# A transformer stack on one core: rounded output product within one turn, one buffer for the heads' outputs, Gelu from PSUM, keys copied once and placed by two transfers

## What is computed

```python
def attn_layer(x, Wqkv, qs, ksc, Wo):          # x is shift_tokens(x); 16 heads of 64
    q, k, v = heads(x @ Wqkv)
    q = rotary(l2norm(q) * qs);  k = rotary_inv(l2norm(k) * ksc)
    sim = einsum('bhwie,bhwje->bhwij', bq, bk2) * 8.0        # windows of 32, causal
    out = einsum('bhwij,bhwje->bhwie', softmax(mask(sim)), bv2)
    return out.reshape(b, n, 1024) @ Wo

def ffn_layer(x, g, bln, W1, b1, W2, b2):      # x is shift_tokens(x)
    xn = (x - mu) / jnp.sqrt(var + 1e-05) * g + bln
    a, gate = jnp.split(xn @ W1 + b1, 2, -1)    # 341 + 341
    return a * gelu(gate) @ W2 + b2
```

## Time and profile before

| what | value |
|---|---|
| median of 3 runs | 3024.75 us (3023.71 to 3027.78) |
| the profiled execution | 3025.93 us, its span 3024.1 us |
| busy in the span | PE 94%, DVE 79%, ACT 80%, POOL 70% |
| the layers | first projection matmul 406.2 us, last 2933.3 us |

### The profile page before, as it was taken

One profiled execution on the slowest core, in us unless ns is written; L12 is line 12 of the kernel. 1 busy time (PEld: TensorE's weight loads), 2 busy tenths in 40 slices (PEclk: granted clock), 3 DMA queues, 4 the chain that ended last, 5 costly groups with the idle time before them and its releaser, 6 DMA issues. The chain is left out here.

```text
span 3024.1 us, 90067 instructions
## 1 busy us (share of the span) xinstructions
PE 2847.9 (94%) x34784; PEld 1995.9 (66%) x34976; DVE 2396.9 (79%) x3168; ACT 2423.9 (80%) x3783; POOL 2114.6 (70%) x1517
## 2 busy tenths in 40 slices
PE   8799978999999999999999999999999999999995
PEld 7688856666666666666666666666666666666662
DVE  7899967887787888778788787877788787887872
ACT  5788858788887878888788888878888887888872
POOL 6767657777677777777777777777777776777760
PEclk9899989999999999999999999999999999999997
DMA  1000011100111010010001111000110100100002
GB/s 51 22 1 1 1 33 26 27 23 20 27 32 30 23 26 24 21 41 24 23 23 26 28 31 26 23 23 24 30 31 23 26 23 25 28 21 20 18 21 64
DMA packets 73039, 76.57 MB, mean 25 GB/s; under 512 B 23078, under 2 KB 46692, under 8 KB 72804
## 3 DMA queue, kind: packets, MB, share of 16 engines
q1 hardware_dynamic: 71780, 74.01, 9.5%
q10 hardware_dynamic: 1152, 1.20, 0.1%
HBM read 22.72 MB, written 2.10 MB: 8 GB/s over the span
## 5 line engine op out<-in xcount | busy, mean ns | idle before, releaser
L1313 POOL TENSOR_TENSOR qk_r<-qk_r,qk_t 128x1024 f32<-128x1024 f32 x384 | 917.9, 2391 | 549.9 <-DVE qk_r L1169 387.9
L776 PE MATMUL pa<-w_hi,xs_hi 128*128 128x512 f32 x1152 | 576.2, 500 | 41.1 <-DVE qk_r L1169 24.8
L1162 DVE TENSOR_REDUCE ss<-sq 128x16 f32<-128x1024 f32 x384 | 463.6, 1207 | 19.0 <-ACT sq L959 18.2
L1178 DVE TENSOR_TENSOR qk_t<-pa,rot 128x1024 f32<-128x1024 f32 x384 | 465.5, 1212 | 0.0
L1169 DVE TENSOR_TENSOR qk_r<-pa,rot 128x1024 f32<-128x1024 f32 x384 | 465.5, 1212 | 0.0
L804 PEld LDWEIGHTS px<-ident_sb,qk_r 128*128 128x128 f32 x3072 | 352.3, 141 | 164.6 <-issue 100.5
L776 PE MATMUL pa<-w_hi,xs_lo 128*128 128x512 f32 x1152 | 456.5, 396 | 0.0
L776 PE MATMUL pa<-w_lo,xs_hi 128*128 128x512 f32 x1152 | 454.6, 395 | 0.0
L804 PE MATMUL px<-ident_sb,qk_r 128*128 128x128 f32 x3072 | 402.8, 274 | 30.4 <-POOL qk_r L1322 14.4
L1012 ACT COPY kT<-px 64x1024 f32<-64x1024 f32 x384 | 385.2, 1003 | 34.5 <-PE px L804 29.8
L1322 POOL TENSOR_TENSOR qk_r<-qk_r,inv 128x1024 f32<-128x1024 f32 x192 | 365.9, 1906 | 43.8 <-ACT inv L996 43.5
(11 more groups left out here) (142 smaller groups left out, 5344.4 us busy)
## 6 DMA issues: line engine op xcount, KB each, us to landing
pT<-prT SPq DMA_DIRECT2D x768, 64.0 KB, 2.0
w_part<-in_Wqkv SPq DMA_DIRECT2D x40, 192.0 KB, 2.7
wo<-in_Wo SPq DMA_DIRECT2D x6, 512.0 KB, 4.5
c_h<-in_x SPq DMA_DIRECT2D x4, 512.0 KB, 9.9
o_x<-in_x SPq DMA_DIRECT2D x8, 256.0 KB, 4.8
out<-o_out SPq DMA_DIRECT2D x8, 256.0 KB, 4.3
w<-in_W SPq DMA_DIRECT2D x6, 341.0 KB
spare<-in_Wqkv SPq DMA_DIRECT2D x1, 1536.0 KB, 6.3
```

Source lines behind the costliest of these rows:

```text
L776: last = pe.matmul(pa[(u + c) % 2][:, half * 512:half * 512 + 512], x[:, j * P:(j + 1) * P], w[:, at], start=(k == 0), stop=(k == 2))
L1162: dve.reduce_sum(ss[:, c, :], heads(sq[:]), AX.X).then_inc(s[sum_sem], 1)
L1178: dve.tensor_tensor(halves(qk_t[:, c, :]), halves(pa[(3 * j + c) % 2][:])[:, :, ::-1, :], table.unsqueeze(1).to_broadcast([P, HEADS, 2, DH ...
L1313: pool.tensor_tensor(qk_r[:, j % 2, c, :], qk_r[:, j % 2, c, :], qk_t[:, c, :], ALU.add)\
```

## The change

What it does, part by part:

- **Output product.** `Wo` is split once a layer in `wo_hi` (ACT, `round_wo`) and `wo_lo` (POOL, `rest_of_wo`). ACT's copy of the heads' outputs now rounds into `oT_hi`; a new step on DVE, `rest_of_outputs`, subtracts it from `px` and writes `oT_lo`. `project_out` has for each of its eight pairs of heads three float32r matmuls in place of one float32 matmul. `px` is free for the next transposes when both have read it (`oT_lo_ready`).
- **One buffer.** `oT_hi` and `oT_lo` hold one group in place of two. The values `v` and the rotated `qk_r` move into the room `spare` that `oT` had.
- **Gelu from PSUM.** The gate's three copies with bias become three Gelu with bias, straight from `pg`; the Gelu over `gt` goes. The tables for Gelu are asked for ahead of the first, those for exp and ln behind the third.
- **Keys.** ACT copies the transposed keys once, in full rows, to `k_both`; SP places them with two transfers of 64 rows and 4 KB a row, 256 KB each, into `kT`, whose layout is now halves first; `scores` waits for these.
- **Feed-forward.** The tiles `fsq`, `frs`, `fn` are one tile `fx`; the square is taken from PSUM; `scale_shift` moves from ACT to DVE.
- **Order.** Every engine's `body` is written anew. On PE `scores` comes after `project_q`, and `weigh_values` before `project_v`. `group_steps` writes out the first two groups of every layer. `w_part` has one buffer in place of two. PE no longer waits at the start for all cleared tiles.

The core of the diff, for all engines, SP and PE:

```diff
         def group_steps(eng, body, new_layer):
-            new_layer(0)
-            body(0, 0, 0)
-            body(1, 0, 1)
-            with eng.Fori(2, GROUPS) as g:
-                body(g, 0, g)
-            for l in range(1, DEPTH):
+            for l in range(DEPTH):
                 new_layer(l)
-                with eng.Fori(0, GROUPS) as g:
+                for g in range(2):
+                    body(g + l * GROUPS, l, g)
+                with eng.Fori(2, GROUPS) as g:
                     body(g + l * GROUPS, l, g)
...
+                def place_keys(i, j, back):
+
+                    n, _, live = tile(i, j, back)
+                    if live:
+                        sp.wait_ge(s["tk_out"], n + 1)
+                        wait_for(sp, s["scores_done"], n)
+                        for half in range(2):
+                            rows = slice(half * DH, (half + 1) * DH)
+                            sp.dma_start(kT[rows, half].rearrange("p h b j -> p (h b j)"), k_both[rows, :])\
+                                .then_inc(s["kT_ready"], 16)
+
                 def body(i):
                     for j in range(GT):
...
+                        place_probs(i, j, 3)
+                        place_keys(i, j, 1)
...
-                        wait_for(pe, s["pv_out"], n - 2)
+                        wait_for(pe, s["oT_lo_ready"], n - 2)
                         transposes(j, 0, "tq_done")
...
                         for hp in range(lo, hi):
-                            heads_out = oT[:, bass.ds(g % 2, 1), hp, :, :].rearrange("p o t n -> p (o t n)")
-                            last = pe.matmul(pg[:], wo[:, hp, :], heads_out, start=(hp == 0), stop=(hp == HP - 1))
+                            for k, (w, o) in enumerate(((wo_hi, oT_hi), (wo_hi, oT_lo), (wo_lo, oT_hi))):
+                                last = pe.matmul(pg[:], w[:, hp, :], o[:, hp, :, :].rearrange("p t n -> p (t n)"),
+                                                 start=(hp == 0 and k == 0), stop=(hp == HP - 1 and k == 2))
...
-                pe.wait_ge(s["mask_ready"], 2)
-                pe.wait_ge(s["zeroed"], 8)
                 group_steps(pe, body, lambda l: None)
```

The order of a turn on PE, as written now (turn by turn `j`):

```diff
+                        if j == 2:
+                            a_block(i, 2, 1)
                         project_q(i, j, l)
+                        if j == 0:
+                            subtract_mean(i, 2)
+                        scores(i, j, 2)
+                        transpose_q(i, j, 1)
+                        if j == 2:
+                            a_block(i, 2, 2)
                         if j == 1:
+                            gate_block(i, 2, 0)
+                        project_k(i, j, l)
+                        if j == 1:
+                            gate_block(i, 2, 1)
+                        if j == 3:
+                            project_out(i, 1, 0, HP // 2)
+                        transpose_k(i, j, 1)
+                        if j == 3:
+                            project_out(i, 1, HP // 2, HP)
+                        if j == 1:
+                            gate_block(i, 2, 2)
                         if j == 2:
+                            down(i, 2)
+                        if j == 0:
+                            variance(i, 2)
+                        weigh_values(i, j, 3, 1)
                         if j == 1:
+                            a_block(i, 2, 0)
                         project_v(i, j, l)
```

On ACT, the key copy, the Gelu and the order of a turn:

```diff
-                        for half in range(2):
-                            rows = slice(half * DH, (half + 1) * DH)
-                            act.copy(kT[rows, :, :, half, :].rearrange("p h b j -> p (h b) j"),
-                                     px[rows, :].rearrange("p (h j) -> p h j", j=S)).then_inc(s["tk_out"], 1)
...
+                        wait_for(act, s["kT_ready"], 32 * n)
+                        act.copy(k_both[:], px[:]).then_inc(s["tk_out"], 1)
...
-                        act.activation(gt[0:m, k, :], pg[0:m, :], ACT.Identity, bias=b1[0:m, 1, k:k + 1])\
+                        act.activation(gt[0:m, k, :], pg[0:m, :], ACT.Gelu, bias=b1[0:m, 1, k:k + 1])\
                             .then_inc(s["gate_out"], 1)
...
+                        if isinstance(g, int) and g == 1 and l < DEPTH and j == 0:
+                            round_wo(l)
+                        copy_v(i, j, 1)
+                        square_q(i, j, 0)
+                        log_norms(i, j, 1)
+                        inverse_norms(i, j, 1)
+                        if j == 0:
+                            shift_hi(i, 0, 1)
                         if j == 1:
+                            tables(i, 2, GELU)
+                        if j == 0:
+                            square_centred(i, 2)
+                        if j == 1:
+                            gate_gelu(i, 2, 0)
+                        copy_qT(i, j, 1)
+                        if j == 0:
+                            copy_centred(i, 2)
+                        square_k(i, j, 0)
+                        if j == 1:
+                            gate_gelu(i, 2, 1)
+                        copy_kT(i, j, 1)
+                        if j == 0:
+                            log_variance(i, 2)
+                            inverse_deviation(i, 2)
+                        if j == 1:
+                            gate_gelu(i, 2, 2)
+                            tables(i, 2, EXP_LN)
+                        exponentials(i, j, 2)
+                        if j == 3:
+                            shift_ffn(i, 1)
+                        if j == 1:
                             round_part(l, g)
...
+                        copy_oT(i, j, 3)
+                        floor_norms(i, j, 0)
```

On DVE the new step, and on POOL the order of a turn:

```diff
+                def rest_of_outputs(i, j, back):
+                    n, k, live = tile(i, j, back)
+                    if live:
+                        dve.wait_ge(s["pv_out"], n + 1)
+                        dve.tensor_tensor(oT_lo[:, :, k, :].rearrange("p h (r q) -> p r h q", r=2),
+                                          px[:].rearrange("p (r h q) -> p r h q", r=2, h=HP),
+                                          oT_hi[:, :, k, :].rearrange("p h (r q) -> p r h q", r=2).bitcast(F32), ALU.subtract)\
+                            .then_inc(s["oT_lo_ready"], 1)
...
+                        if j == 3:
+                            shift_lo(i, -1, 0)
+                        norm_keys(i, j, 1)
                         if j == 3:
                             rest_of_part(l, g)
...
+                        norm_scores(i, j, 2)
+                        if j == 1:
+                            shift_lo(i, 0, 1)
+                        rotate(i, j, 0, 0, "cos_q", "sin_q", "rot_q")
+                        rotate(i, j, 0, 1, "cos_k", "sin_k", "rot_k")
+                        norm_probs(i, j, 2)
```

450 lines of the change are left out of this document (204 added, 246 removed).

## The result

| what | before | after |
|---|---|---|
| median | 3025.34 us (4 runs, 3023.71 to 3027.78) | 2975.72 us (4 runs, 2974.20 to 2978.85) |
| span of the profiled execution | 3024.1 us | 2973.8 us |
| a group of the loop | 52.60 us | 51.63 us |

The ratio is 0.9838, 95% interval 0.9822 to 0.9853: 1.6% faster, 49.6 us. A second set of five runs on another chip gave 0.9840 (0.9827 to 0.9854). The forecast was 2930, 95 us less than before; its range held the time, its size was off by almost half. 0.97 us a group times 48 is 47 us, so nearly all of it was won in the loop; how it splits is at the end of the account of the prediction.

What follows compares the result with a forecast made beforehand. PE was taken as the bound, at 49.4 us of work a group. A group of 50.6, 2.0 less, gives 96 us (64 product, 32 order); with 1 off the start and 4 back, 2930 us, range 2885 to 2990.

Steps and rivals of the forecast that it cites:

- PE is the bound, and the product saves 1.34 us a group: Output product on PE: 24 float32r matmuls take 5.5 us where 16 records took 6.9; 64 us over 48 groups.
- ahead of each product with the values, with no releaser: PE's small waits before the values' matmuls, read as 0.16 us each; 0.3 a group added to the walk's sum.
- only the product pays: Rival: PE idle stays 1.9 us or more, the keys' copy being on each turn's path; 2962 to 2985; chance 0.24.
- the one that had 0.55: Main forecast band: PE bound with waits of about 1.2 us a group, 2890 to 2950 us.
- The new order loses no time and wins 32 us: Order of steps in the loop: 32 of the 96 us gained there were put down to the order.
- the walk of turn 0: Step-by-step timing of the group's first turn: 10.8 us, PE waiting 0.4; all four turns sum to 50.3.
- the lag of DVE from turn to turn: Named greatest risk: DVE has 3.7 us to spare in 50.6, and a wait there returns in each later turn.
- 64 us for the product: Output product's share of the 96 us forecast to be gained in the loop, from 1.34 us a group.
- DVE is second and not the bound: DVE with the 1.13 us subtraction comes to 46.9 us a group, under PE's 49.4.
- The keys' transfer is hidden, by 0.4 us at the worst place: SP's second key transfer takes 3.3 us, lands at 11.8; scores start at 12.2, in turn 1.
- the keys come late: Rival: scores wait for the key transfer and the kernel slows; 3112 us at L = 6; chance 0.06.
- it breaks even at L = 5.4: L, second key transfer's issue to landing: at 5.4 the scores' waits use up the 2.0 us a group gain.

Runs made afterwards that it cites:

- e5: Kernel after with the output product as one float32 matmul per head pair instead of three float32r: ratio 0.9961, 3015.88 us.
- e7: Kernel after with DVE's subtraction for the rest of the outputs cut to 64 columns of one head pair, other rests zeroed once: ratio 0.9813.
- e3: Kernel after with add_attention ahead of the denominators on DVE in turn 3: ratio 0.9737, 2948.39 us.
- e10: Kernel after with ACT's copy of the heads' outputs ahead of shift_ffn in turn 3: ratio 0.9780.
- e2: Kernel after with ACT's shift_hi of turn 0 moved behind the norm of the feed-forward part: ratio 0.9792.
- e6: Kernel after with the second transfer of the keys issued only when the first has landed: ratio 1.0095, 3052.69 us.
- e8: Kernel after with the keys placed by two half-row ACT copies, without whole-row copy or transfer: ratio 1.0117, 3060.75 us.
- e12: Kernel after with scores ahead of the projection of q on PE again, as before the change: ratio 1.0503, 3179.09 us.
- e1: Kernel after with ACT's copy of the transposed q moved ahead of shift_hi and square_centred in turn 0: ratio 0.9899.

## Why the prediction was right in sign and short in size

**PE is the bound, and the product saves 1.34 us a group: right.** Output matmuls are 0.23 us apart in the kernel after. Between two heads PE is busy for 50.55 us a group in e5 and 49.15 in e7, whose PE does the same work as the kernel after; both traces lack the mask's record. The difference is 1.4. But the work of a group was not the 50.7 us from which I subtracted, for two reasons. The 0.16 us "ahead of each product with the values, with no releaser" was the mask's matmul without a record: 28.1 us, 0.64 a group. And the window of the earlier trace rows holds the head of a layer, a group of 56.3 us in which PE stands idle for 4.8, so scaling the window's busy time by 52.6 in 700 gives too little. One group between two heads, before and after (length, then PE, PEld, DVE, ACT, POOL):

```profile
1505.73:1558.33 52.60, 51.13 (x688) 34.77 (x691) 42.39 (x50) 44.21 (x62) 38.38 (x25) 1.00 0.09 24
```

```profile
1532.86:1584.46 51.60, 50.05 (x713) 36.23 (x706) 47.08 (x56) 38.91 (x56) 38.35 (x26) 1.00 0.26 65
```

So PE's work before was 51.1 + 0.6 = 51.8 and its idle time 0.8; after, they are 50.1 and 1.5. The work fell by 1.7, 1.4 of it by the product; the other 0.3 came with the rest of the change, and no run takes it apart. That the work "becomes 49.4 us a group" was too low by 0.7, and that PE's idle time falls, from 1.9 to 1.2, was wrong: it rose, from 0.8 to 1.5. The rival "only the product pays" added that 49.4 to the 1.9 of idle time; its two faults cancel, and its 2962 to 2985 is where the time fell. So the time lies in the range of the forecast, but in the band that had a chance of 0.24 and not in the one that had 0.55.

**The new order loses no time and wins 32 us: wrong.** This is the step that failed: the walk of turn 0. The walk's turns against the starts of the turns in the timeline after (1495.06, 1507.74, 1520.63, 1534.76, 1546.68):

| turn | walk | measured |
|---|---|---|
| 0 | 10.8 | 11.92 |
| 1 | 12.4 | 12.68 |
| 2 | 13.0 | 12.89 |
| 3 | 14.1 | 14.13 |

Of the 1.3 us that are missing, 1.1 are in turn 0. The matmuls were summed nearly right, 49.9 us against the 50.1 measured; what is short is the waiting, 0.7 with what was added for waits without a releaser, against 1.5. The walk let ACT begin turn 0 free: "ACT's square of q ends at 2.4, the norms at 2.9". In the timeline they end 3.4 and 4.1 after the turn's start, because `shift_ffn` and the copy of the heads' outputs of turn 3 come first, 2.3 us of ACT's work that begins 1.04 before the turn does. The walk had "PE waits 0.4" in turn 0; it is 1.27. That this lateness is what costs was shown by taking it away: e3 (31 us), e10 (18) and e2 (14) each shorten the series at another place, and each gives time, and in e3 and e10 the wait for `qT` goes from 31.7 us to 2.7 and 15.4. I named the lag of DVE from turn to turn as what I would be most wrong by. It was a lag from one turn to the next, but of ACT, set off by two steps of DVE, and only in one turn of four.

**The size of the product's term.** Of 64 us for the product, 37 are there (e5). The rest is not a mis-sized duration: of the 1.4 us that PE is spared, 0.67 is the wait for `qT` that e5 does not have. Without the cover of the longer product the same lateness of ACT shows in turn 0.

**DVE is second and not the bound: right.** The subtraction takes 1.19 us by its row against 1.13 taken, and DVE's work is 47.1 against 46.9. Cutting it to a sixteenth is worth 8 us (e7), and nothing in a steady group. ACT's 38.7 against 37.5 is the larger miss; part of it is the same window (44.2 us in the group above, not 43.8).

**The keys' transfer is hidden, by 0.4 us at the worst place: right.** I took 3.3 us for the second and let it land 3.9 after the first issue; the rows give 3.7, and 4.3 after the first issue, and the scores wait for it 0.09 a group. The estimate from the Trainium skill (SBUF — State Buffer, "Can I just issue two DMAs to hit both halves?") was 4.4 us from the first issue for both; the trace is nearer to it than to my value. The rival "the keys come late" was tried by e6: 5.8 after the first issue is an L of about 5.2, for which its formula gives 1.5 + 0.1 = 1.6 us of waits a group, in turns 1 and 3, and 1.7 are seen. Only "it breaks even at L = 5.4" was wrong, since the gain to be used up was 1.0 a group and not 2.0: e6 is 27 us slower than before.

**The parts don't add.** The single copy of the keys with its transfers, seen from e8, is worth 84 us, the product, seen from e5, 37, and undoing the exchange costs 201; together they gave 49.6. Each figure is the price of taking one part out of an order that is built on it. The whole order without its product is worth about 12 us (49.6 - 37), where I had 32.

**Start, heads of the layers and drain.** The first projection starts at 402.3 us against 406.2, 3.9 earlier where I took 1. By the starts of `add_attention`, eight groups with the head of a layer among them take 424.4 us before and 415.2 after: 9.2 less, where eight times 0.97 is 7.8. So each of the five heads gave about 1.4 us, 7 in all, where I had 3.6 of loss. The 0.6 us that I took for rounding `Wo` is there: at the head of a layer PE waits 1.18 and 0.68 us where it waits 0.75 and 0.52 in other groups. But the kernel before waits at this place for POOL's scaled keys, up to 1.79 us, and the kernel after does not. Between the last two `add_attention`, in the drain, lie 44.4 us in place of 41.3, 3.1 lost. That leaves some 42 of the 49.6 us for the other groups.

## What stays open

PE still waits 0.69 us a group for the keys' copy ahead of the mask, with all the edits. In turns 0 and 1 too little stands between, and no kernel here tried to put more there. The 0.1 us that a block of projections costs when it is split is read from single turns of e12's timeline. The 0.3 us a group of PE's work that went beside the product's 1.4 were not traced to a part of the change.

## What to carry to other kernels

- When you walk the turns of a pipeline, start each engine where its last turn left it, not at the start of the turn. An engine with a quarter of its time to spare can still be the late one in the turn behind its busiest.
- An engine that runs a series without a gap and ends in a wait of the bound engine is not helped by exchanging the steps of the series (e1), but by an earlier start of it or by fewer steps ahead of the one waited for. Look one engine further back: here two small instructions of DVE ahead of the one that ACT waited for cost 31 us.
- Before a window's busy time is scaled to a group, see whether the window holds a group that is not like the others. Here one such group in 700 us took 0.4 us off PE's work of a group.
- An idle time with no releaser, the same length each time and at the same place, may be an instruction without a record. Count the weight loads against the matmuls before it goes into the sum as a wait.
